# A graph attention kernel: two of 128 adjacency half loads issued as 120 and 8 partitions

## The chip, the cores and the metric

The kernel runs on one core of one Trainium2 chip. The metric is the device time of one execution in microseconds (us). The core has five engines (TensorE, VectorE, ScalarE, GpSimd and SyncE; in the profile PE with its weight loads PEld, DVE, ACT, POOL and SP) and sixteen DMA engines that move data between HBM and the on-chip memory.

## The reference

One layer of graph attention over 8192 nodes with 128 features. `adj` is an int32 matrix of 8192 x 8192, 256 MiB, in which about one entry in 2048 is 1, so a row has some four neighbours.

```python
h = jnp.maximum(_layernorm(x, axis=-1), 0.0)
s_i = h @ attn[:128]
s_j = h @ attn[128:]
e = leaky_relu(s_i + s_j.T, negative_slope=0.2)
e = e + jnp.where(adj > 0, 0.0, -1e9)
out = x + softmax(e, axis=1) @ h
```

## The kernel before

The rows are split into 64 tiles of 128 rows (`TILES`); row `64 p + t` lies on partition p of tile t. Two tiles make a pair (`PAIRS` = 32). The kernel first normalises `x`, writes a table of rows of h to HBM, and then streams the adjacency matrix once, finding each row's few neighbours and gathering only their rows of the table.

A tile of the adjacency matrix is loaded in two halves of 4096 columns. A half load is 128 partitions x 16,384 bytes, 2 MiB; there are 128 of them, numbered n = 2 t + h. They go into a ring of five slots, `adj_ring` (`HALVES` = 5, slot n % 5), each slot with a DMA semaphore of its own, `adj_in[n % 5]`, to which one DMA adds 16 when all of it has landed. All the half loads are issued by SyncE, in `load_pair` (L410 to 415), in order. Before load n it waits until ScalarE has signed half n - 5 (L413). On the same queue, in program order, stand the stores of the finished pairs (`store_pair`, L417 to 421).

ScalarE, in `sign_tile` (L606 to 615), waits for half n to land (L609), writes its sign as one byte per element into `sign_ring` (four slots), which frees the slot of `adj_ring`, and counts `signed` up. TensorE packs the signs into words in PSUM (`pack_tile`, L1366), VectorE finds the largest words of each chunk (L769) and from them the neighbours' numbers `near_id`; GpSimd gathers the neighbours' rows (`gather_pair`, L521, twelve indirect DMAs a pair), and VectorE scores, weighs and sums them (L906 to L957). Every eight pairs a list of rows with many neighbours is treated in a like manner (`near_m`, L532). After the last half has been signed comes a closing part: the last pairs, the rows without any neighbour (128 matmuls at L1442), and the last stores.

Of the kernel before, what the change touches and what calls it, by code (L numbers as in the profile page):

```python
# [5 lines left out]
def graph_attention_kernel(nc: bass.Bass, x: bass.AP, adj: bass.AP, attn: bass.AP, out: bass.AP):  # L6
# [6 lines left out]
    P = 128  # L13
# [3 lines left out]
    HALF = N // 2  # L17
# [15 lines left out]

    DIGITS = CHUNKS // 2
    HALVES = 5
    SHIFTS = [3 * (c // 2) + 2 * (c % 2) for c in range(CHUNKS)]
    EACH = sum(8 ** d for d in range(DIGITS)) * WORDS
    UNIT = 11.0
# [49 lines left out]

    def early_parts(k):
        return [c for c in range(LONE_PARTS[0]) if PART_AT[c] == k]  # L90

    table = nc.dram_tensor("h_table", [N + 1, COLS], fp32).ap()

# [3 lines left out]
    adj_t = adj.rearrange("(p t) c -> t p c", p=P)  # L97
# [3 lines left out]
    with ctx:  # L101
        def sb(name, shape, dt):
            return ctx.enter_context(nc.sbuf_tensor(name, shape, dt))
# [4 lines left out]
        def sem(name):  # L108
            return ctx.enter_context(nc.semaphore(name))

        adj_ring = sb("adj_ring", [P, HALVES, HALF], i32)
        sign_ring = sb("sign_ring", [P, 4, HALF], fp8)
# [179 lines left out]
        attn_in = sem("attn_in")  # L292
        adj_in = [sem(f"adj_in{i}") for i in range(HALVES)]
        consts = sem("consts")
# [107 lines left out]
        @block.sync  # L402
        def _(sp):
            for c in range(XC):
                sp.dma_start(x_all[:, c * XT:(c + 1) * XT, :], x_t[:, c * XT:(c + 1) * XT, :]).then_inc(x_in[c], 16)
                if c == 0:
                    sp.dma_start(attn_b[:, :], attn.rearrange("d o -> o d").broadcast_to([P, 2 * D])) \
                        .then_inc(attn_in, 16)

            def load_pair(p):  # L410
                for n in range(4 * p, 4 * p + 4):
                    if n >= HALVES:
                        sp.wait_ge(signed, n - HALVES + 1)  # L413
                    sp.dma_start(adj_ring[:, n % HALVES, :], adj_t[n // 2, :, (n % 2) * HALF:(n % 2 + 1) * HALF]) \
                        .then_inc(adj_in[n % HALVES], 16)

            def store_pair(g):  # L417
                sp.wait_ge(pair_mixed, g + 1)
                if g >= 2:
                    sp.wait_ge(stored[g % 2], 16 * (g // 2))  # L420
                sp.dma_start(out_t[:, 2 * g:2 * g + 2, :], x_all[:, 2 * g:2 * g + 2, :]).then_inc(stored[g % 2], 16)

            load_pair(0)
            load_pair(1)
            for p in range(2, PAIRS):
                load_pair(p)
                for g in MIXES.get(p - 2, []):
                    store_pair(g)
            for g in range(PAIRS - 4, BODY + 1):
                store_pair(g)  # L430

            sp.wait_ge(sizes_ready, 2)
            tiles = sp.value_load(far_tiles[0:1, 0:1], min_val=1, max_val=TILES)
            parts = sp.value_load(far_parts[0:1, 0:1], min_val=1, max_val=DC)
            with sp.Fori(0, tiles) as t:
                with sp.Fori(0, parts) as c:
                    sp.wait_ge(far_used, DC * t + c + 1)
                    sp.sem_inc(sp_passed, 1)
                    sp.dma_start(far_h, table[ds(c * DW + 1, DW), :].rearrange("(k q) c -> q k c", q=P)) \
                        .then_inc(far_h_in, 16)  # L440
                    sp.dma_start(far_adj, adj_t[ds(t, 1), :, ds(c * DW, DW)].rearrange("o p w -> (o p) w")) \
                        .then_inc(far_adj_in, 16)
                    sp.wait_ge(far_free, DC * t + c + 1)
                    sp.sem_inc(sp_passed, 1)
                    sp.dma_start(far_x, x_t[:, ds(t, 1), :].rearrange("p o d -> p (o d)")).then_inc(far_x_in, 16)

        @block.gpsimd
        def _(pool):
# [24 lines left out]
            for c in range(CHUNKS):  # L473
                nc.gpsimd.memset(code_mask[:, c:c + 1], 2 ** SHIFTS[c] * WORDS + WORDS - 1)
            nc.gpsimd.memset(fill[:, :], SKIP)
# [127 lines left out]
        def _(act):  # L603
            act.wait_ge(consts, 1)

            def sign_tile(t, halves=(0, 1)):  # L606
                for h in halves:
                    n = 2 * t + h
                    act.wait_ge(adj_in[n % HALVES], 16 * (n // HALVES) + 16)  # L609
                    if n >= 4:  # L610
                        act.wait_ge(packed, n - 3)
                    bytes_of = sign_ring[:, n % 4, :].rearrange("p (d i r) -> p d r i", d=DIGITS // 2, r=2)
                    nc.scalar.activation(bytes_of, adj_ring[:, n % HALVES, :].rearrange("p (d r i) -> p d r i", r=2, i=WORDS),  # L613
                                         ACT.Sign, bias=half_neg[:, :], saturate=False,
                                         accum_out=degree[:, t, h:h + 1]).then_inc(signed, 1)
# [45 lines left out]
            root_quarter(2)  # L661
            root_quarter(3)
            sign_tile(0)
            relu_quarter(2)
            sign_tile(1)
            def exp_lone(b, c):
                part = lone_p[b][c % len(lone_p[b])]
# [3 lines left out]
            def exp_step(p):  # L671
                for g in MIXES.get(p, []):
                    exp_pair(g)
                for c in early_parts(p - 1 - FIRST_STEP):
                    exp_lone(0, c)

            for p in range(1, PAIRS):
                sign_tile(2 * p, (0,))
                exp_step(p - 1)
                sign_tile(2 * p, (1,))  # L680
                sign_tile(2 * p + 1, (0,))
                if p >= SEG and p % SEG == DEEP_MIX:
                    exp_m(p // SEG - 1)
                sign_tile(2 * p + 1, (1,))
# [31 lines left out]
        def _(dve):  # L716
# [432 lines left out]
            def lone_add(c):  # L1149
                n = LONE_MARK + LONE_HOT + LONE_IDS  # L1150
                acc = lone_acc[0:LONE_CAP[0], :]
                dve.wait_ge(lone_summed[0], early_parts(c)[-1] + 1)
                if c == 0:
                    nc.vector.tensor_copy(acc, lone_sum[0]).then_inc(lone[0], 1)
                else:
                    dve.wait_ge(lone[0], n + c)
                    nc.vector.tensor_tensor(acc, acc, lone_sum[0], ALU.add).then_inc(lone[0], 1)
# [29 lines left out]
            def lone_close(p):  # L1187
                for c in early_parts(p - FIRST_STEP):
                    lone_part(0, c)
# [358 lines left out]
```

## Time and profile before

| | us |
|---|---|
| median of 3 runs | 821.86 |
| lowest, highest | 820.19, 822.15 |
| span of the profiled execution | 819.9 |
| VectorE busy | 615.3 |
| ScalarE busy | 534.3 |
| GpSimd busy | 505.0 |
| TensorE busy | 379.5 |

The span is the time from the first to the last instruction of one profiled execution. Its views are: busy time by engine and stretch, with the mean busy share of the sixteen DMA engines and the GB/s that they moved; the chain of work that ended last, followed back from the end; who waited for whom; the DMA queues and issues; and the instructions in order of time. In them "x" before a number is a count. An idle time is put down to what ended it. The profile doesn't tell the sixteen DMA engines apart: it gives their mean share and their sum.

### The profile page before, as it was taken

The numbers are of one execution on the slowest core, as the hardware profiler recorded it, in microseconds if no ns is written. First come the engines' busy times: TensorE is split into PE (matmuls) and PEld (weight loads), VectorE is DVE, ScalarE is ACT, GpSimd is POOL, SyncE is SP. The second block draws the span as 40 slices with busy tenths as digits, with TensorE's granted clock in tenths as the row PEclk, the third lists the DMA queues.
The fourth block names the chain that finished last, engine by engine and source line by source line (L and its number), as shares of the span: only waits on it lengthen the run. The fifth ranks groups of instructions, "written<-read, shape, count | busy, mean of one in ns | idle before, by whom it ended". The sixth has DMA issues, their size and how long they took to land.

```text
span 819.9 us, 6412 instructions
## 1 busy us (share of the span) xinstructions
PE 379.5 (46%) x1378; PEld 171.4 (21%) x1378; DVE 615.3 (75%) x2028; ACT 534.3 (65%) x410; POOL 505.0 (62%) x526
## 2 busy tenths in 40 slices
PE   1546334444444344344343434444434546653765
PEld 1322011111111011111111101111111215431654
DVE  6898298677768667797778666697689799897831
ACT  4975676676676666766766666676676677764620
POOL 6720777755457767665547677555557667655771
PEclk9776665555555555555555555655555556766768
DMA  8999999999999999999999999999999999981210
GB/s 341 402 411 415 392 404 408 406 414 413 409 407 410 408 405 410 406 410 410 412 406 407 408 406 407 411 410 413 412 413 409 408 411 407 409 348 43 53 37 4
DMA packets 39719, 301.59 MB, mean 368 GB/s; under 512 B 10682, under 2 KB 17149, under 8 KB 22272
## 3 DMA queue, kind: packets, MB, share of 16 engines
q1 hardware_dynamic: 24032, 277.04, 83.1%
q0 software_dynamic: 15360, 23.88, 8.5%
q10 hardware_dynamic: 288, 0.26, 0.1%
q8 instruction: 11, 0.18, 0.1%
q14 instruction: 28, 0.23, 0.1%
HBM read 303.76 MB, written 8.98 MB: 381 GB/s over the span
## 4 chain that ended last, share of the span: by engine, by line
DMA 76%; issue 11%; DVE 5%; ACT 4%; PE 3%; POOL 0%; DVEq 0%; ACTq 0%
DMA adj_ring<-in_adj_dram 75%; ACT sign_ring L613 3%; PE words L1442 2%; DVE one_hot L724 1%; ACT h_all L625 1%; PE words L1406 1%; DMA x_all<-in_x_dram 1%; PE words L1366 0%; DVE cand L769 0%; DVE adj_ring L1142 0%; DVE adj_ring L1138 0%; DVE adj_ring L1146 0%; PE words L1516 0%; POOL out_dram L562 0%; ACT terms L620 0%
## 5 line engine op out<-in xcount | busy, mean ns | idle before, releaser
L613 ACT ACTIVATE sign_ring<-adj_ring,half_neg 128x4096 fp8e3<-128x4096 int32 x128 | 474.9, 3710 | 217.1 <-DMA adj_ring<-in_adj_dram 215.4
L521 POOL DMA_INDIRECT near<-h_table,near_id x384 | 391.8, 1020 | 235.4 <-issue 122.8
L1366 PE MATMUL words<-sign_ring,pack_w 128*128 128x512 bf16 x512 | 225.2, 592 | 354.8 <-ACT sign_ring L613 354.8
L769 DVE MAX8 cand<-words 128x8 f32<-128x256 f32 x256 | 90.9, 417 | 115.4 <-PE words L1366 115.4
L1366 PEld LDWEIGHTS words<-sign_ring,pack_w 128*128 128x128 bf16 x512 | 55.0, 127 | 521.9 <-ACT sign_ring L613 451.6
L954 DVE TENSOR_REDUCE sums<-terms 128x128 f32<-128x1024 f32 x58 | 112.2, 1934 | 2.0
L532 POOL DMA_INDIRECT near_m<-h_table,id_m x64 | 64.5, 1008 | 19.5 <-issue 19.2
L949 DVE TENSOR_TENSOR terms<-near,weight 128x512 f32<-128x512 f32 (+1 forms) x87 | 73.4, 871 | 0.0
L1357 PE MATMUL words<-place,place_w 128*128 128x512 bf16 x128 | 62.1, 586 | 3.6 <-DVE key L861 3.6
L1392 PEld LDWEIGHTS listing<-cand,one_hot 128*128 128x128 f32 x128 | 33.6, 321 | 10.9 <-issue 7.7
L1347 PE MATMUL listing<-h_all 128*1 128x128 f32 x128 | 19.1, 322 | 22.8 <-ACT h_all L625 22.8
L1392 PE MATMUL listing<-cand,one_hot 128*128 128x34 f32 x128 | 28.0, 362 | 0.2 <-DVE one_hot L865 0.2
L613 ACT ACTIVATION_READ_ACCUMULATOR sign_ring<-adj_ring,half_neg 128x1 f32 x128 | 23.8, 186 | 0.0
L1442 PE MATMUL rank<-h_all,x_all 128*64 128x129 f32 x128 | 21.1, 344 | 4.6 <-DVE key L861 4.6
L786 DVE TENSOR_TENSOR terms<-cand_i,code_mask 128x512 int32<-128x512 int32 x32 | 22.2, 693 | 1.1
L957 DVE SCALAR_TENSOR_TENSOR x_all<-sums,inv,x_all 128x128 f32<-128x128 f32 x58 | 20.4, 352 | 2.1
L643 ACT ACTIVATE adj_ring<-ident,adj_ring 128x128 f32<-128x128 f32 x48 | 14.4, 387 | 11.1 <-DVE adj_ring L969 11.1
L755 DVE TENSOR_TENSOR near<-h_all,terms 128x2048 f32<-128x2048 f32 x8 | 21.5, 2686 | 0.0
L1442 PEld LDWEIGHTS rank<-h_all,x_all 128*64 128x64 f32 x128 | 20.3, 182 | 4.9 <-DVE key L861 4.9
L498 POOL TENSOR_SCALAR h_all<-x_all,terms 128x128 f32<-128x128 f32 x16 | 13.0, 830 | 11.7 <-DVE terms L741 11.7
L625 ACT ACTIVATE h_all<-x_all,terms 128x128 f32<-128x128 f32 x48 | 18.8, 479 | 2.1 <-DVE terms L741 2.1
L906 DVE TENSOR_SCALAR score<-near,h_all 128x8 f32<-128x8 f32 x32 | 7.3, 228 | 17.1 <-DMA near<-h_table,near_id 17.1
(271 smaller groups left out, 524.3 us busy)
## 6 DMA issues: line engine op xcount, KB each, us to landing
adj_ring<-in_adj_dram SPq DMA_DIRECT2D x128, 2048.0 KB, 24.6
near<-h_table,near_id POOLq DMA_INDIRECT x384, 6.4
h_table<-h_all POOLq DMA_DIRECT2D x4, 1056.0 KB, 14.7
x_all<-in_x_dram SPq DMA_DIRECT2D x4, 1024.0 KB, 9.4
out_dram<-x_all SPq DMA_DIRECT2D x30, 128.0 KB, 23.9
near_m<-h_table,id_m POOLq DMA_INDIRECT x64, 6.4
out_dram<-x_all ACTq DMA_DIRECT2D x2, 128.0 KB, 2.5
adj_ring<-h_table SPq DMA_DIRECT2D x1, 132.0 KB, 2.6
```

Source lines behind the costliest of these rows:

```text
L521: pool.indirect_dma_start(out=near[:, p % RING, k, :], out_offset=None, in_=table, in_offset=bass.IndirectOffsetOnAxis(ap=near_id[:, p % I ...
L532: pool.indirect_dma_start(out=near_m[:, k, :], out_offset=None, in_=table, in_offset=bass.IndirectOffsetOnAxis(ap=id_m[:, k:k + 1], axis=0 ...
L613: nc.scalar.activation(bytes_of, adj_ring[:, n % HALVES, :].rearrange("p (d r i) -> p d r i", r=2, i=WORDS), ACT.Sign, bias=half_neg[:, :] ...
L625: nc.scalar.activation(h_all[:, t, 0:D], x_all[:, t, :], ACT.Relu, bias=shift[:, t:t + 1], scale=rstd[:, t:t + 1]).then_inc(h_ready, 1)
L769: last = nc.vector.max(out=cand[:, p % 2, t % 2, 8 * q:8 * q + 8], in_=words[t % 3][:, q * PART:(q + 1) * PART])
L786: nc.vector.tensor_tensor(codes[:, :, :, :].rearrange("p a w c -> p (a w) c"), cand_i[:, :, :].rearrange("p a w -> p (a w)").unsqueeze(2). ...
L949: nc.vector.tensor_tensor(terms[:, at, :], near[:, e, slots, 0:D], weight[:, g % 2, weights].unsqueeze(2).broadcast_to([P, at.stop - at.st ...
L954: nc.vector.tensor_reduce(sums[:, a, :], terms[:, :, :].rearrange("p k d -> p d k"), AX.X, ALU.add).then_inc(mixing, 1)
L1357: nc.tensor.matmul(at[:, k * BANK:(k + 1) * BANK], place_w[:, :], place[:, k * BANK:(k + 1) * BANK], start=True, stop=False)
L1366: last = nc.tensor.matmul(at[:, k * BANK:(k + 1) * BANK], pack_w[:, d, :], twins[:, o + k * BANK:o + (k + 1) * BANK], start=False, stop=(d ...
L1392: last = nc.tensor.matmul(listing[:, 0:REC], one_hot[:, p % 2, a, :], cand[:, p % 2, a, :], start=(p % SEG == 0 and a == 0), stop=(p % SEG ...
L1442: last = nc.tensor.matmul(lone_sum[b], part[:, k * e:(k + 1) * e], h_all[:, c * lt + k, 0:ONE + 1], start=(first and k == 0), stop=(final ...
```

## The change

Half loads 52 and 104 are issued as two DMAs each: one of partitions 0 to 119 and one of partitions 120 to 127, with the same columns, the same slot and the same semaphore. Each adds 16 to the semaphore, so the value that ScalarE waits for is no longer 16 a load but 16 for each DMA of that slot up to and with load n (`landed`). The other 126 loads, their order and all the compute instructions are the same.

```diff
     HALVES = 5
+    SPARED = (52, 104)
+    WIDE = 120
...
+    def landed(n):
+        return 16 * sum(2 if k in SPARED else 1 for k in range(n % HALVES, n + 1, HALVES))
...
                     if n >= HALVES:
                         sp.wait_ge(signed, n - HALVES + 1)
-                    sp.dma_start(adj_ring[:, n % HALVES, :], adj_t[n // 2, :, (n % 2) * HALF:(n % 2 + 1) * HALF]) \
-                        .then_inc(adj_in[n % HALVES], 16)
+                    columns = slice((n % 2) * HALF, (n % 2 + 1) * HALF)
+                    for rows in ((slice(0, WIDE), slice(WIDE, P)) if n in SPARED else (slice(0, P),)):
+                        sp.dma_start(adj_ring[rows, n % HALVES, :], adj_t[n // 2, rows, columns]) \
+                            .then_inc(adj_in[n % HALVES], 16)
...
-                    act.wait_ge(adj_in[n % HALVES], 16 * (n // HALVES) + 16)
+                    act.wait_ge(adj_in[n % HALVES], landed(n))
```

## Rows read from the trace of the kernel before

**Rows 1.** The page's chain that ended last: share of the span by line.

```profile
DMA adj_ring<-in_adj_dram 75%; ACT sign_ring L613 3%; PE words L1442 2%; DVE one_hot L724 1%; ACT h_all L625 1%; PE words L1406 1%; DMA x_all<-in_x_dram 1%; PE words L1366 0%; DVE cand L769 0%; DVE adj_ring L1142 0%; DVE adj_ring L1138 0%; DVE adj_ring L1146 0%; PE words L1516 0%; POOL out_dram L562 0%; ACT terms L620 0%
```

**Rows 2.** The same chain in order of time: start us, us, what.

```profile
93.30 24.48 DMA adj_ring<-in_adj_dram
117.80 3.81 ACT sign_ring L613 x2
...
719.76 3.81 ACT sign_ring L613 x2
723.59 23.35 DMA adj_ring<-in_adj_dram
746.96 3.81 ACT sign_ring L613 x2
...
810.92 0.98 POOL out_dram L562
```

**Rows 3.** ScalarE in order of time, 463 to 500: start, duration, idle before.

```profile
475.08 3.71 ACT L613 ACTIVATE sign_ring<-adj_ring,half_neg 128x4096 fp8e3<-128x4096 int32 x1 [1.72 <-DMA adj_ring<-in_adj_dram]
...
482.00 3.71 ACT L613 ACTIVATE sign_ring<-adj_ring,half_neg 128x4096 fp8e3<-128x4096 int32 x1 [3.11 <-DMA adj_ring<-in_adj_dram]
...
487.42 3.71 ACT L613 ACTIVATE sign_ring<-adj_ring,half_neg 128x4096 fp8e3<-128x4096 int32 x1 [1.51 <-DMA adj_ring<-in_adj_dram]
...
492.89 3.71 ACT L613 ACTIVATE sign_ring<-adj_ring,half_neg 128x4096 fp8e3<-128x4096 int32 x1 [1.67 <-DMA adj_ring<-in_adj_dram]
```

**Rows 4.** Groups of instructions by line, 120 to 720: the signs.

```profile
L613 ACT ACTIVATE sign_ring<-adj_ring,half_neg 128x4096 fp8e3<-128x4096 int32 x107 | 397.1, 3711 | 191.3 <-DMA adj_ring<-in_adj_dram 189.6 <-PE words L1366 1.7
```

**Rows 5.** Busy time by stretches: engines, granted PE clock, DMA share, GB/s.

```profile
core 0: us, PE busy (x) PEld busy (x) DVE busy (x) ACT busy (x) POOL busy (x), PEclk, DMA share, GB/s
60.00:100.00 40.00, 18.74 (x56) 7.06 (x57) 22.78 (x86) 23.91 (x13) 14.93 (x16) 0.63 1.01 404
100.00:200.00 100.00, 42.83 (x116) 14.49 (x114) 78.60 (x259) 68.05 (x41) 67.81 (x66) 0.55 1.01 409
...
500.00:600.00 100.00, 42.40 (x116) 13.91 (x116) 74.64 (x261) 68.06 (x44) 55.49 (x57) 0.55 1.01 411
600.00:700.00 100.00, 52.70 (x199) 26.62 (x199) 90.43 (x274) 71.18 (x43) 72.82 (x70) 0.54 1.01 409
700.00:734.00 34.00, 18.02 (x75) 11.44 (x76) 31.05 (x104) 23.17 (x16) 21.59 (x22) 0.67 1.01 406
```

**Rows 6.** The page's DMA issues: count, KB each, median us to landing.

```profile
adj_ring<-in_adj_dram SPq DMA_DIRECT2D x128, 2048.0 KB, 24.6
```

**Rows 7.** DMA from 726 to 750 us in 40 slots of 0.6.

```profile
GB/s 420 410 368 364 404 394 495 410 375 387 403 336 354 311 200 167 128 63 41 32 133 27 90 60 25 90 27 99 27 71 27 56 27 214 67 46 21 21 92 0
```

**Rows 8.** Busy time by stretches around the last loads, columns as in rows 5.

```profile
724.00:728.00 4.00, 1.50 (x4) 0.29 (x2) 3.74 (x19) 3.02 (x3) 3.09 (x4) 0.50 1.02 408
728.00:732.00 4.00, 1.92 (x6) 0.72 (x6) 3.62 (x14) 1.81 (x3) 1.70 (x2) 0.50 1.00 403
732.00:736.00 4.00, 3.40 (x18) 3.40 (x19) 3.83 (x21) 3.19 (x3) 0.02 (x1) 0.55 0.69 280
736.00:738.00 2.00, 2.00 (x19) 1.71 (x18) 1.90 (x8) 1.51 (x1) 1.08 (x2) 1.00 0.13 51
...
sum 24.00, PE 14.11 PEld 8.17 DVE 22.62 ACT 16.66 POOL 13.75; mean PE 1.57 PEld 0.91 DVE 2.51 ACT 1.85 POOL 1.53
```

**Rows 9.** DMA queues from 474 to 484: packets, MB, share of 16 engines.

```profile
q1 hardware_dynamic: 263, 3.74, 92.6%
q0 software_dynamic: 245, 0.29, 8.3%
q14 instruction: 1, 0.01, 0.2%
```

**Rows 10.** The same from 480 to 500.

```profile
q1 hardware_dynamic: 656, 7.65, 93.9%
q0 software_dynamic: 458, 0.48, 7.0%
q14 instruction: 1, 0.01, 0.1%
```

**Rows 11.** The page's DMA queues of code: packets, MB, share.

```profile
q8 instruction: 11, 0.18, 0.1%
q14 instruction: 28, 0.23, 0.1%
```

**Rows 12.** One line's instructions, L414: ns of one, minimum, median, maximum.

```profile
L414 SPq DMA_DIRECT2D adj_ring<-in_adj_dram x128: 327/328/629, 3.3 to 723.6; - x128
```

**Rows 13.** What SyncE's queue waited for: us in total, times, longest.

```profile
SPq L414 <- ACT sign_ring L613: 639.7, 121, 22.8
```

**Rows 14.** The head of the page.

```profile
span 819.9 us, 6412 instructions
```

## Prediction

> **What bounds the kernel now.** I read the chain of waits first. Three quarters of the span is one line, the landing of `adj_ring` [rows 1]; in order of time it alternates between about 24 us of waiting for a half load and one sign on ScalarE that frees the next slot of the ring [rows 2]. The sign is short beside the wait, 3.71 us of every period [rows 3]. From the sign at 117.80 to the one at 719.76 ScalarE signs 107 halves [rows 4], so 106 periods take 601.96 us, 5.68 us each [rows 2].
>
> The next view is the busy time by stretches. From 60 to 734 us the sixteen DMA engines are occupied all the time (share 1.01) and move 404 to 411 GB/s. VectorE is busy some 75 to 79 us of 100, and 90 of 100 from 600 to 700 [rows 5]. So what the load stage waits for is the DMA engines' own work, not an issue, a buffer or a compute engine. A load is issued 24.6 us before it lands (median) [rows 6], more than four periods of 5.68 us: an engine has a queue of transfers ahead of it, and one that falls behind isn't starved, it just stays behind.
>
> The third view is the end of the loads, and it is the one that matters here. Twelve slots of 0.6 us show near 400 GB/s; between 734 and 737 the rate falls to 32, and from there to 745.8 the floor is 27 GB/s, with short peaks of gathers on top [rows 7]. One sixteenth of 408 is 26, so that floor is one engine working alone, for about 9 us, while fifteen have finished. The mean share says the same: 1.02, 1.00, 0.69, then 0.13 from 736 to 738 [rows 8]. The last sign can't start before 746.96 [rows 2]. Since all sixteen get equal parts of each load, this engine carries something besides. The signs show what: from 475.08 to 482.00 the period is 6.92 us, 1.24 over the mean [rows 3], and the stretch from 474 to 484 holds one 8 KB packet of queue 14, instruction code [rows 9]. In 480 to 500, behind that one, there is another such packet [rows 10], and the periods stay at 5.42 and 5.47 us [rows 3]. So a code fetch lies on one engine, and only some of them on the engine that is last. Seven or eight at 1.24 us make the 9 us; the page counts 28 and 11 fetches in all [rows 11]. The pace of the kernel is that of this one engine, which I call the last engine.
>
> After 746.96 comes a chain of 73 us to the end with no adjacency load in it [rows 2]. What the last load gains or loses moves that chain whole.
>
> **The change part by part.** *Issue.* Two more DMAs on SyncE's queue. One takes 0.33 us [rows 12], so 0.66 us in all. SyncE waits 639.7 us for signs [rows 13]; behind each issue stand only the next loads and the stores of results, and a load is issued some 20 us before it is due. Cost on the path: nothing, hidden by the queue of transfers; without that cover it would be 0.66 us.
>
> *The wait.* ScalarE waits for 16 more on the semaphore of that slot. It is the same instruction with another number, for the same bytes. Nothing, as long as both parts land together.
>
> *The wide part.* 120 rows of 16 KB divide evenly over fifteen engines, eight rows each, and not over sixteen. I take it that one engine gets none. An engine alone moves 27 GB/s [rows 7], so a row of 16,384 bytes costs it 0.61 us and eight rows 4.85 us. If the one left out is the last engine, it is relieved of 2 x 4.85 = 9.7 us.
>
> *The narrow part.* Eight rows on eight engines, one each: 0.61 us for each of those eight, twice, 1.2 us. If the last engine is among them, 1.2 us on the path.
>
> The Trainium skill, "DMA: Bandwidth & Descriptors", section "Why a DMA increments its semaphore by 16 and not by 1", says that a DMA from SyncE runs on the largest number of engines up to 16 that divides its slowest dimension, and that these are the lowest-numbered; by that, 120 rows leave out the highest-numbered engine and the eight rows use the lowest eight. No run here shows it yet. The section "Latency and other measured facts" calls engines 7 and 15 usually slower, which would make the one left out the right one; the trace agrees that one engine is last, but has no number for it, and ties its lag to code fetches. "SBUF — State Buffer", "Door 1: The DMA port swizzle", speaks against the change: eight partitions in two groups of four share a port of some 27 GB/s, and a full load gives each engine its own port. By that rule the upper bound above would be the likely value, and the sum for an unrelieved last engine would be 12.1 us instead of 6.1.
>
> **The sum.** No row names the engine that is last, or the one that 120 rows leave out. They are two of sixteen, and the fetches are spread over more than one engine [rows 3, 9, 10], so I don't count on their being the same. Then the last engine keeps its eight rows in both wide parts, gets one more row in each narrow part (1.2 us), and writes among others' partitions (4.9 us): 6.1 us later at the last sign, and at the end. The profiled execution, span 819.9 us [rows 14], stands 2.0 us under the median of 821.86, the launch around it included. 821.9 + 6.1 = 828.0 us.
>
> **The rivals.** *A, the forecast: the last engine isn't relieved.* Price 0 to +12.1 us (1.2 + 10.9), so 821.9 to 834.0. For it: nothing in the profile points at the one left out. Against it: the relief of 9.7 us fits the 9 us of lag.
>
> *B, the last engine is the one left out, and the sharing costs little.* It would be done 9.7 us earlier; then the second-latest sets the end, which [rows 7] puts 9 us ahead, plus up to 1.2 for the narrow rows. Gain 8 to 9 us; VectorE, busy 22.6 of the 24 us before 748 [rows 8], may keep back 1 or 2 of it. So 812.9 to 815. It decides when the wide part costs the other fifteen less than some 2 us: they have only those 9 us in hand. For it speaks the size of the lag; against it, that sixteen engines could be meant.
>
> *C, left out, but the sharing gives it back.* The other fifteen are 9 us ahead and pay 1.2 + 4.9 to 1.2 + 10.9 us; the sum is -3 to +3 us against now, 819 to 825.
>
> *D, the change doesn't do what it says:* both parts are spread over all engines anyway, or the eight rows lie on engines that have slack. Then 821.9, within A's and C's range.
>
> **How the numbers follow.** Two executions of this kernel can be told apart from about 0.3%, 2.5 us, so "same" is 819.4 to 824.4. A has a chance of 0.55, of which 0.12 within 2.5 us (little sharing, D with it) and 0.43 slower. B has 0.27, all faster. C has 0.18: 0.04 faster, 0.09 same, 0.05 slower. Together faster 0.31, same 0.21, slower 0.48. The likeliest case is A, 828.0; its own range is 822 to 834. B is too likely to leave out, so the range goes down to 812.5; up it goes to 834.
>
> **What would show it.** The view of the end of the loads, as in [rows 7], tells the cases apart. In B the floor of 27 GB/s is gone or under 2 us and the last sign starts near 738 to 739. In A the floor is as long or longer and the last sign starts at 748 or later. In C there is no floor, but the fall comes late, near 745 to 749. Sharing would show as longer periods of the signs around halves 52 and 104 (near 322 and 616 us): in A one period of 5.68 us becomes 8 to 11, in C the periods lengthen only where the slack is used up. The wait of ScalarE for `adj_ring`, and nothing on VectorE or TensorE, should take up the difference. The prediction is wrong if the left-out engine is the last one, or if the tail behind the last load doesn't move with it.

## The result and the profile after

The changed kernel takes 846.22 us (843.86 to 850.58, 4 runs) against 821.63 us (820.19 to 822.15, 4 runs): 1.0301 of the time before, 95% interval 1.0278 to 1.0324. It is 24.6 us slower, and above the range of the prediction. The profiled execution has a span of 842.1 us, 22.2 us over that of before.

The page first: the GB/s of the span in 40 slices of 21 us, and the count, MB and share of SyncE's DMA queue.

```profile
GB/s 345 405 405 419 401 406 405 410 411 411 410 402 412 407 363 291 408 413 414 415 415 405 408 409 407 412 411 412 369 259 353 406 407 402 408 352 46 50 37 5
q1 hardware_dynamic: 24046, 277.04, 82.9%
```

Two dents stand in a row that is flat otherwise, at slices 15 and 16 (295 to 337 us) and 29 to 31 (589 to 653 us), where half loads 52 and 104 pass. The queue has as many MB as before and 14 packets more. One load on sixteen engines has 128 rows and 16 semaphore writes; in 120 + 8 it has the same 128 rows and 15 + 8 writes, 7 more, 14 for two loads. (The column split below, with two more DMAs of 128 rows, has 288 packets more, 144 each.) So the wide part did run on fifteen engines and the narrow one on eight, as the Trainium skill, "DMA: Bandwidth & Descriptors", section "Why a DMA increments its semaphore by 16 and not by 1", has it.

The same dents by stretches (columns as in rows 5: busy time of each engine, granted PE clock, DMA share, GB/s):

```profile
290.00:312.00 22.00, 9.27 (x25) 3.26 (x26) 14.52 (x53) 14.73 (x10) 15.02 (x15) 0.50 1.03 399
312.00:326.00 14.00, 4.06 (x10) 1.02 (x9) 4.27 (x13) 6.05 (x4) 10.91 (x11) 0.50 1.00 219
326.00:340.00 14.00, 3.24 (x10) 0.64 (x7) 8.59 (x30) 6.43 (x4) 7.49 (x8) 0.62 1.00 370
...
606.00:624.00 18.00, 4.26 (x13) 1.93 (x14) 14.69 (x54) 8.33 (x7) 12.24 (x12) 0.55 1.03 220
```

The DMA share stays at 1.00 while the rate is 219 GB/s, against the 404 to 411 of [rows 5]: on the mean every engine is occupied, and its packets take nearly twice as long. The kernel before has 412 GB/s from 312 to 326. In slots of 1.2 us, first from 296 to 344 and then from 592 to 640, the dents have clear edges:

```profile
GB/s 393 442 381 419 412 397 406 385 424 437 423 311 365 188 219 235 249 234 232 198 203 190 229 219 236 257 253 352 386 401 366 410 404 392 410 414 363 443 385 394
```
```profile
GB/s 425 384 412 393 424 387 422 387 410 408 405 396 257 248 218 194 264 225 218 186 221 147 226 200 151 230 200 207 345 442 339 402 385 373 403 378 355 363 410 374
```

The rate is halved for 14 slots, 16.8 us from 311.6, and for 16 slots, 19.2 us from 606.4. From 290 to 340 the changed kernel moves 22 x 399 + 14 x 219 + 14 x 370 = 17.0 thousand GB/s x us, that is 17.0 MB; at the 409 of a normal stretch it would be 20.5. The missing 3.4 MB are 8.4 us of work.

ScalarE's signs show where it lands (start, duration, idle before); these are halves 50 to 53:

```profile
310.45 3.71 ACT L620 ACTIVATE sign_ring<-adj_ring,half_neg 128x4096 fp8e3<-128x4096 int32 x1 [1.22 <-DMA adj_ring<-in_adj_dram]
320.70 3.71 ACT L620 ACTIVATE sign_ring<-adj_ring,half_neg 128x4096 fp8e3<-128x4096 int32 x1 [6.45 <-DMA adj_ring<-in_adj_dram]
332.52 3.71 ACT L620 ACTIVATE sign_ring<-adj_ring,half_neg 128x4096 fp8e3<-128x4096 int32 x1 [8.02 <-DMA adj_ring<-in_adj_dram]
337.48 3.71 ACT L620 ACTIVATE sign_ring<-adj_ring,half_neg 128x4096 fp8e3<-128x4096 int32 x1 [1.05 <-DMA adj_ring<-in_adj_dram]
```

In the kernel before they start at 310.88, 316.37, 322.20 and 327.89. So sign 50 is on time, sign 51 is 4.3 us late although load 51 isn't cut, sign 52 is 10.3 and sign 53 9.6 us late. The delay then shrinks to 8.4 us by sign 99. Around the second cut it goes to 15.7 (sign 102), 19.0, 26.0 (sign 104) and settles at 22.9, which is also the delay of the last sign (769.87 against 746.96).

The end of the loads, 750 to 774 us in slots of 0.6, to be set against [rows 7]:

```profile
GB/s 443 350 440 416 483 292 359 338 167 157 82 27 27 27 34 27 27 27 77 84 27 123 7 108 27 99 27 65 34 25 31 210 93 27 46 0 113 0 97 0
```

The floor of 27 GB/s is still there. It runs from 756.6 to 768.6, 12.0 us; counted in the same way it was 8.4 us before, from 737.4 to 745.8 in [rows 7]. At 27 GB/s one engine is alone as before, and it is further behind. The 73 us behind the last sign [rows 2] are 72.2 us now: the delay is passed on whole. ScalarE's wait for `adj_ring` takes up the difference: 239.2 us in all, was 215.4. TensorE's and VectorE's longer waits follow from it: TensorE waits 379.9 us for signs (was 354.8), and VectorE 126.9 us for TensorE's words (was 115.4).

### The profile page after: what moved, and what is told of

Its sections match the earlier page's. It is cut to its first block, busy times and chain, and to the rows that moved or that the text cites. A ratio compares the mean times of both kernels' runs of the same rounds, so it can differ in the third digit from the quotient of the medians.

```text
span 842.1 us, 6395 instructions
## 1 busy us (share of the span) xinstructions
PE 371.0 (44%) x1359; PEld 170.2 (20%) x1378; DVE 614.7 (73%) x2028; ACT 534.2 (63%) x410; POOL 503.9 (60%) x526
## 4 chain that ended last, share of the span: by engine, by line
DMA 70%; issue 13%; DVE 5%; POOL 4%; ACT 3%; PE 3%; DVEq 0%; POOLq 0%; ACTq 0%
DMA adj_ring<-in_adj_dram 66%; POOL near L528 4%; ACT sign_ring L620 2%; DVE near L762 2%; PE words L1449 2%; DMA h_table<-sums 2%; DMA near<-h_table,near_id 1%; DVE one_hot L731 1%; ACT h_all L632 1%; PE words L1413 1%; DMA x_all<-in_x_dram 1%; DVE h_all L767 0%; PE words L1373 0%; DVE cand L776 0%; PE words L1523 0%
## 5 line engine op out<-in xcount | busy, mean ns | idle before, releaser
L620 ACT ACTIVATE sign_ring<-adj_ring,half_neg 128x4096 fp8e3<-128x4096 int32 x128 | 474.9, 3710 | 239.2 <-DMA adj_ring<-in_adj_dram 239.2
L1373 PE MATMUL words<-sign_ring,pack_w 128*128 128x512 bf16 x511 | 220.9, 583 | 380.1 <-ACT sign_ring L620 379.9
L776 DVE MAX8 cand<-words 128x8 f32<-128x256 f32 x256 | 90.9, 417 | 126.9 <-PE words L1373 126.9
L539 POOL DMA_INDIRECT near_m<-h_table,id_m x64 | 64.4, 1006 | 19.5 <-issue 19.2
L1364 PE MATMUL words<-place,place_w 128*128 128x512 bf16 x110 | 55.3, 588 | 7.8 <-DVE key L868 4.4
L1399 PEld LDWEIGHTS listing<-cand,one_hot 128*128 128x128 f32 x128 | 32.7, 314 | 10.6 <-issue 7.2
L1354 PE MATMUL listing<-h_all 128*1 128x128 f32 x128 | 19.1, 322 | 24.6 <-ACT h_all L632 24.6
L793 DVE TENSOR_TENSOR terms<-cand_i,code_mask 128x512 int32<-128x512 int32 x32 | 22.2, 693 | 1.1
L964 DVE SCALAR_TENSOR_TENSOR x_all<-sums,inv,x_all 128x128 f32<-128x128 f32 x58 | 20.4, 352 | 2.1
L632 ACT ACTIVATE h_all<-x_all,terms 128x128 f32<-128x128 f32 x48 | 18.8, 479 | 2.2 <-DVE terms L748 2.2
L913 DVE TENSOR_SCALAR score<-near,h_all 128x8 f32<-128x8 f32 x32 | 7.2, 224 | 17.5 <-DMA near<-h_table,near_id 17.5
```

What stands on the lines that cost most here:

```text
L539: pool.indirect_dma_start(out=near_m[:, k, :], out_offset=None, in_=table, in_offset=bass.IndirectOffsetOnAxis(ap=id_m[:, k:k + 1], axis=0 ...
L632: nc.scalar.activation(h_all[:, t, 0:D], x_all[:, t, :], ACT.Relu, bias=shift[:, t:t + 1], scale=rstd[:, t:t + 1]).then_inc(h_ready, 1)
L776: last = nc.vector.max(out=cand[:, p % 2, t % 2, 8 * q:8 * q + 8], in_=words[t % 3][:, q * PART:(q + 1) * PART])
L1364: nc.tensor.matmul(at[:, k * BANK:(k + 1) * BANK], place_w[:, :], place[:, k * BANK:(k + 1) * BANK], start=True, stop=False)
L1373: last = nc.tensor.matmul(at[:, k * BANK:(k + 1) * BANK], pack_w[:, d, :], twins[:, o + k * BANK:o + (k + 1) * BANK], start=False, stop=(d ...
L1399: last = nc.tensor.matmul(listing[:, 0:REC], one_hot[:, p % 2, a, :], cand[:, p % 2, a, :], start=(p % SEG == 0 and a == 0), stop=(p % SEG ...
```

## The experiments

They ran in four sessions, for which the record names four chips (15, 3, 0 and 6). On each the kernel before takes 834 to 835 us instead of 821.6. It falls behind the first measurement step by step: 7.2 us at sign 50, 15.1 at sign 99 and 16.4 at the end. The medians are set against the runs of the kernel before in the same session (835.15, 835.05, 835.05 and 834.07 us). The signs are set against one profile of it, taken on chip 3. The table gives how late a sign starts against that profile, in us. Also with no cut these levels wander, by up to 8 us (a kernel with no cut stands at -8.2 at sign 101). Over four or five signs with no cut they move by 2.7 us at most. So the jumps across a cut count, not the levels.

| kernel | sign 50 | 54 | 101 | 106 | 127 |
|---|---|---|---|---|---|
| changed kernel (a2_after) | 2.8 | 13.4 | 8.6 | 20.4 | 21.5 |
| split by columns (e3) | -0.3 | 1.2 | -2.2 | -0.6 | -0.1 |
| 120 alone (e4) | -0.9 | 7.3 | 1.3 | 15.1 | 15.2 |
| 112 + 16 (e6) | -0.2 | 8.0 | 6.6 | 18.8 | 18.3 |
| 64 + 64 (e5) | 0.4 | 12.1 | 7.0 | 19.6 | 18.8 |
| other source rows (e7) | 0.5 | 8.8 | 4.2 | 18.2 | 17.5 |
| only 52 cut (e1) | 1.5 | 11.3 | 3.1 | 2.8 | 3.3 |
| only 104 cut (e2) | 0.3 | -0.6 | -3.3 | 11.1 | 10.3 |

**The reference profile.** The kernel before, unchanged.

> The kernel before, unchanged, profiled on the chip of the experiments, so that the signs of the others can be set against it half by half. 835 us if the chip is the one of the first experiments, 822 if it is like that of the first measurement.

836.79 us, span 835.0.

**The changed kernel on this chip.** No edit.

> The changed kernel itself on the chip of the experiments (where the kernel before takes 835 us). If both cuts have the price seen in the single cuts there: signs late by 11 us behind 52, falling to some 3 to 5 before 102, then 13 us more; 851 to 857 at the end. The difference to the kernel without the eight rows (late by 15 us at the end) is the price of the narrow part: 1 to 4 us.

857.33 us, ratio 1.0251 (1.0192 to 1.0309). The price is the same in kind and size, 23.3 us. Before the second cut comes, the delay has fallen to 6.3 (sign 99) and 8.6 us (sign 101) and not to 3 to 5, and the second jump is 11.8 us and not 13; both are within what the levels wander by.

**Two DMAs, but equal parts.**

```diff
-    WIDE = 120
+    CUT = 3840
...
-                    for rows in ((slice(0, WIDE), slice(WIDE, P)) if n in SPARED else (slice(0, P),)):
-                        sp.dma_start(adj_ring[rows, n % HALVES, :], adj_t[n // 2, rows, columns]) \
+                    base = (n % 2) * HALF
+                    for a, b in (((0, CUT), (CUT, HALF)) if n in SPARED else ((0, HALF),)):
+                        sp.dma_start(adj_ring[:, n % HALVES, a:b], adj_t[n // 2, :, base + a:base + b]) \
```

> Half loads 52 and 104 are again issued as two DMAs each on one semaphore, but split by columns: 128 partitions x 3840 columns and 128 partitions x 256 columns. Same bytes, same number of issues, same waits, and every engine keeps its equal part and its partitions. Theory 1 (the price is that fifteen engines write partitions that others write as well): no change against the kernel before, 821.6 within 1 us. Theory 2 (the price is the second issue, its semaphore or the shared wait): the whole 24.6 us of the changed kernel comes back, 846.

836.92 us against 835.15, ratio 1.0026 (1.0003 to 1.0048). The second issue, the shared semaphore and the longer wait cost 1.8 us for both loads together (0.3 to 4.0 by the interval), and a part of that may be the short rows of 1 KB. That is over the 1 us of theory 1, and far from the 24.6 of theory 2, which falls.

**The wide part alone.**

```diff
-        return 16 * sum(2 if k in SPARED else 1 for k in range(n % HALVES, n + 1, HALVES))
+        return 16 * sum(1 for k in range(n % HALVES, n + 1, HALVES))
...
-                    for rows in ((slice(0, WIDE), slice(WIDE, P)) if n in SPARED else (slice(0, P),)):
+                    for rows in ((slice(0, WIDE),) if n in SPARED else (slice(0, P),)):
```

> Of half loads 52 and 104 only partitions 0 to 119 are loaded; partitions 120 to 127 of these two halves keep what the slot held before (so the output of those rows is another one). Theory 1 (the price lies in the 120-partition DMA): 840 to 846, the signs behind half 52 late by 7 to 10 us and behind half 104 by 18 to 23. Theory 3 (the eight rows of the narrow DMA, eight engines on few partitions, are the costly part): 822 to 830.

852.71 us, ratio 1.0206 (1.0168 to 1.0243). The 120 rows carry 17.6 us, a little under the 18.4 to 24.4 of theory 1, and the second jump left the signs 15 us late and not 18 or more. The changed kernel is 23.3 us over its own runs of the kernel before, so the eight rows add 5.7. That is more than their bytes (131 KB a load, 0.3 us at 408 GB/s) and more than the 1 to 4 expected, and a quarter of the price.

**Sixteen engines, other sets.** Cut at 112: seven rows and one row for each of sixteen engines.

```diff
-    WIDE = 120
+    WIDE = 112
```

> The two half loads are cut at partition 112 instead of 120: 112 = 16 x 7 and 16 = 16 x 1 rows, so all sixteen engines have equal parts and none is left out, but the parts are no longer the sets of partitions of a 128-row load. Theory 1 (sharing of partitions): as slow as the changed kernel or nearly, 835 to 850, with the rate halved for some 15 us around both halves. Theory 4 (the price is that one engine is left out and fifteen carry more): no loss, 821.6 within 2 us.

854.89 us, ratio 1.0232 (1.0194 to 1.0270). The queue has 32 packets more than before: both parts have sixteen semaphore writes, so they ran on all sixteen engines. No engine is left out and none has a row more, and the price is there. So it isn't the unequal load.

**Halves of the partitions.** The same edit with 64.

> The two half loads are cut into 64 and 64 partitions. All sixteen engines have four rows in each, but each part covers only half of the partitions. Theory 1 (engines that write partitions of the same group share its rate): the rate falls to about half around both loads and the signs are late by 8 to 15 us at each. If only the unequal split into fifteen mattered: no delay.

857.84 us, ratio 1.0261 (1.0223 to 1.0299), again with 32 packets more. The stretch from 322 to 336 us in the reference, the column split, 112 + 16, 64 + 64 and the one with other source rows, in this order and each from its own profile (columns as above):

```profile
322.00:336.00 14.00, 6.10 (x16) 1.50 (x16) 7.50 (x37) 8.06 (x6) 10.34 (x11) 0.62 1.01 391
```
```profile
322.00:336.00 14.00, 4.99 (x14) 1.38 (x13) 6.39 (x32) 7.71 (x5) 9.95 (x10) 0.62 1.01 352
```
```profile
322.00:336.00 14.00, 4.40 (x12) 1.09 (x10) 3.37 (x17) 3.80 (x2) 9.79 (x10) 0.50 1.02 224
```
```profile
322.00:336.00 14.00, 2.34 (x6) 0.62 (x7) 0.86 (x6) 4.10 (x4) 9.14 (x10) 0.50 1.00 196
```
```profile
322.00:336.00 14.00, 4.68 (x12) 1.23 (x12) 3.92 (x19) 4.20 (x4) 9.97 (x10) 0.50 1.00 217
```

Whenever the rows are cut, the rate is 196 to 224 GB/s with all engines occupied (206 for the changed kernel itself in the same stretch); when the columns are, it is 352, a tenth under the reference's 391. "SBUF — State Buffer", section "Door 1: The DMA port swizzle", of the Trainium skill says that 64 partitions reach eight of sixteen ports of about 27 GB/s, 218 GB/s together. The 196 of the 64 + 64 cut is a tenth under that, and the 217 to 224 of the other cuts sit at the same value. Which ports the engines reach at a time in those cuts no view shows.

**Other rows in HBM.**

```diff
-                        sp.dma_start(adj_ring[rows, n % HALVES, :], adj_t[n // 2, rows, columns]) \
+                        sp.dma_start(adj_ring[rows, n % HALVES, :], (adj[P * (n // 2):P * (n // 2) + P, :][rows, columns] if n in SPARED else adj_t[n // 2, rows, columns])) \
```

> As the changed kernel, but the two cut loads read rows of the matrix that follow each other in HBM (row pitch 32 KB) instead of every 64th row (pitch 2 MB); it computes two half tiles from the wrong rows. Theory 1 (the engines share the SBUF side: partitions written at the same moment): as late as the changed kernel, 9 to 10 and 13 to 15 us. Theory 5 (the rows of one engine collide in HBM because of the 2 MB pitch, now that another set of rows goes together): little or no delay.

856.13 us, ratio 1.0234 (1.0174 to 1.0294), with jumps of 8.4 and 14.0 us. The pitch of the source isn't the cause. With the column split (e3) and the cut at 112 (e6) this leaves the destination: which engine writes which partitions. That is an argument by elimination, since no view separates the engines.

**One cut at a time.** `SPARED = (52,)`, `(104,)`, `(20,)` and `(127,)`.

> Only half load 52 is cut into 120 and 8, load 104 is one DMA. If each cut load has its own price: the signs behind half 52 are late by 9 to 10 us and stay so to the end, 831. If the 14 us of the second one in the changed kernel come from the first one's after-effects (engines further apart), the end is the same 831, and a kernel with only load 104 cut would be late by 9 to 10 as well and not by 14.

> Only half load 104 is cut into 120 and 8. If the price grows with how far the DMA engines have drifted apart (by half 104 the last one is 9 us behind), the signs behind it are late by 13 to 15 us although nothing happened at 52. If the larger second price of the changed kernel came from the first cut, they are late by 9 to 10.

> Only half load 20 is cut, where the DMA engines have hardly drifted apart. If the price grows with the drift: 3 to 7 us late behind it. If it is the same for each cut: 9 to 10. A theory in which the cut relieves the last engine would have it earlier by up to 5 us at the end.

> Only the very last half load, 127, is cut into 120 and 8. When the last engine comes to it, the other fifteen have been done for some 9 to 13 us. If the price is that the last engine's own rows of the cut load meet other engines' writes: nobody is left to meet, 0 to 2 us late. If the price is that the engines ahead write, with their part of the cut load, the partitions on which the last engine still works for earlier halves: signs 125 to 127 late by 4 to 10 us in spite of that.

Only 52: 842.48 us, 1.0094 (1.0059 to 1.0129). Only 104: 848.09, 1.0138 (1.0074 to 1.0201). Only 20: 839.49, 1.0045 (1.0021 to 1.0069). Only 127: 844.63, 1.0124 (1.0085 to 1.0163). The jump across the cut is 9.8 us at 52 and 14.4 us at 104 with nothing at 52. So the larger second price isn't an after-effect of the first cut. At 20 the jump is 8.8 us (1.5 late at sign 18, 10.3 at 22), where I had expected 3 to 7, since the engines should hardly have drifted apart there. At 127 it is 10.6 us (from -4.6 at sign 123 to 6.0). A price that grows with the drift fits the first three and not the last, behind which no load follows; how far the engines are apart was measured at no cut. Most of the price is there at half 20 already.

What stays at the end is another matter. Against the reference profile the delay of the cut at 20 shrinks from 10.3 to 2.0 us by the last sign, and that of the cut at 52 from 11.3 to 3.3. But the seven kernels with no cut up to half 103 also gain 0.8 to 6.1 us on this profile between signs 54 and 99, so much of this is the reference's own. The medians against their own sessions are the better measure: 4.4, 7.3, 13.0 and 10.6 us for the cuts at 20, 52, 104 and 127, against jumps of 8.8, 9.8, 14.4 and 10.6. Of the cut at 20 about half is recovered (1.8 to 5.8 us are left by the interval); for the later ones the intervals don't tell what is left from the whole jump. How an early delay is recovered is open.

The cut at 127 shows that loads that aren't cut are held up too. Signs 124 to 127 of the reference and then of this kernel:

```profile
747.73 3.71 ACT L613 ACTIVATE sign_ring<-adj_ring,half_neg 128x4096 fp8e3<-128x4096 int32 x1 [2.17 <-DMA adj_ring<-in_adj_dram]
752.92 3.71 ACT L613 ACTIVATE sign_ring<-adj_ring,half_neg 128x4096 fp8e3<-128x4096 int32 x1 [1.28 <-DMA adj_ring<-in_adj_dram]
757.96 3.71 ACT L613 ACTIVATE sign_ring<-adj_ring,half_neg 128x4096 fp8e3<-128x4096 int32 x1 [1.24 <-DMA adj_ring<-in_adj_dram]
763.39 3.71 ACT L613 ACTIVATE sign_ring<-adj_ring,half_neg 128x4096 fp8e3<-128x4096 int32 x1 [1.63 <-DMA adj_ring<-in_adj_dram]
```
```profile
744.67 3.71 ACT L620 ACTIVATE sign_ring<-adj_ring,half_neg 128x4096 fp8e3<-128x4096 int32 x1 [3.72 <-DMA adj_ring<-in_adj_dram]
755.59 3.71 ACT L620 ACTIVATE sign_ring<-adj_ring,half_neg 128x4096 fp8e3<-128x4096 int32 x1 [7.01 <-DMA adj_ring<-in_adj_dram]
761.87 3.71 ACT L620 ACTIVATE sign_ring<-adj_ring,half_neg 128x4096 fp8e3<-128x4096 int32 x1 [2.48 <-DMA adj_ring<-in_adj_dram]
769.39 3.71 ACT L620 ACTIVATE sign_ring<-adj_ring,half_neg 128x4096 fp8e3<-128x4096 int32 x1 [3.72 <-DMA adj_ring<-in_adj_dram]
```

From sign 124 to 127 the reference takes 15.66 us, this kernel 24.72. Of the 9.1 us more, 5.7 fall before sign 125 and 7.0 before sign 126, two loads that aren't cut. Only the last 2.1 us come with load 127 itself. A reading that fits is that the engines ahead are in load 127 by then and write, with their part of it, partitions that slower engines are still filling for 125 and 126. That they are the same partitions is argued, since no view shows an engine's own writes.

**Which engine is last.** The kernel before with one more DMA behind load 104, which copies k x 8 rows of 16 KB from HBM to HBM and touches no partition; k = 3, 4, 8, 12 and 15. It was meant to run on k engines. The cut for k = 15; in the others 15 and 120 are k and 8 k:

```diff
+    spare = nc.dram_tensor("spare", [15, 8 * HALF], i32).ap()
...
+        spare_in = sem("spare_in")
...
+                    if n == 104:
+                        sp.dma_start(spare.rearrange("k (m c) -> k m c", m=8), adj[0:120, 0:HALF].rearrange("(k m) c -> k m c", m=8)) \
+                            .then_inc(spare_in, 16)
...
+            sp.wait_ge(spare_in, 16)
```

> As the last, with 3 x 8 rows on three engines. Late by 4.9 us if the pacing engine is one of the three, within 1 us if not. Late with four and not with three would name the fourth engine; late with neither leaves the fifth to the sixteenth.

> As the last, with 4 x 8 rows, so on four engines. If the pacing engine is one of the four that such a DMA uses, late by 4.9 us; if it is another, within 1 us.

> Kernel before with 8 x 8 rows copied within HBM behind load 104, on eight engines. With four engines there was no delay, with fifteen about 5 us. A delay of 4.9 us or more from sign 105 on puts the pacing engine among the fifth to eighth; none puts it among the ninth to fifteenth.

> As the last with 12 x 8 rows on twelve engines. A delay of 4.9 us or more here and none with eight puts the pacing engine among the ninth to twelfth; none here either, among the thirteenth to fifteenth.

> The kernel before with one DMA more behind half load 104: 15 x 8 rows of 16 KB are copied from HBM to a spare place in HBM, which divides over fifteen engines like the wide part, but touches no partition. If the engine that paces the kernel is one of these fifteen, the signs behind half 104 and the end are late by 4.9 us or somewhat more. If it is the one left out, it isn't delayed, and with 5 to 7 us of slack in the others the end stays within 1 us.

The jump from sign 104 to sign 106 is 1.4, 1.5, 2.5, 3.8 and 6.3 us for k = 3, 4, 8, 12 and 15; the medians are 835.04, 835.93, 837.76, 837.13 and 838.88 us, which is 0.0, 0.9, 3.7, 3.1 and 3.8 over the kernel before. The expected picture, nothing and then 4.9 us at once, isn't there, and the packets say why: the edit didn't confine the copy to k engines. SyncE's queue has 36, 48, 80, 112 and 135 packets more than before. Less the 24, 32, 64, 96 and 120 rows that leaves 12, 16, 16, 16 and 15 semaphore writes, one for each engine. So an engine of the copy had 2, 2, 4, 6 and 8 rows, and at 0.61 us a row [rows 7] that is 1.2, 1.2, 2.4, 3.6 and 4.9 us, close to the jumps. The first leaves four engines out, but its 1.4 us is within what the signs wander by. The last leaves one out. Its delay speaks for the last engine being among its fifteen, since the one left out has nothing more to do; but 1.97 MB at 408 GB/s are 4.8 us as well, so it isn't proof. These runs don't name the engine. They show another thing: fifteen engines with eight rows each and no partition to write cost 6.3 us, and the rate doesn't halve (404 GB/s from 624 to 636 and 396 from 636 to 648), where as many rows sent to partitions 0 to 119 halve it.

## Why the prediction was wrong

**The bound of the load stage: right.** The delay of the last sign, 22.9 us, is the delay of the profiled execution (22.2), and in both dents the DMA share is 1.00 or more. (VectorE's 75 to 79 us of 100 were read too narrowly: it is busy 68 to 80 in the stretches from 100 to 600. Nothing hangs on it.)

**Issue and wait: put at nothing, measured 1.8 us (0.3 to 4.0).** The column split has both.

**The parts on fifteen and eight engines: right.** The packet count shows them.

**The last engine isn't relieved: right as far as shown.** The floor of 27 GB/s went from 8.4 to 12.0 us; with 9.7 us taken off that engine and nothing else changed it would have gone. That it is the same engine as before isn't shown. Rival B, 812.9 to 815, is out. So is C as it was put, with at most 3 us over the time before; that an engine was relieved and a much larger price hid it is made unlikely only by the copy on fifteen engines.

**The cause of the lag: supported, not tested.** The prediction tied it to code fetches from a single period. In the kernel before, 12 of the 108 periods between signs 19 and 127 are longer than 6.3 us, and each of the 12 holds a packet of queue 14; the other 96 are 5.54 us on the mean, and some hold such a packet too. No run takes a fetch away.

**The mixing of rows and engines: the right mechanism, the wrong size.** This term failed. The prediction put it at 0 to 10.9 us for both loads and took 4.9, which with 1.2 for the narrow rows made 6.1; the signs jumped by 10 and 14.5 us, 24.6 us at the end. The upper bound was built from the cut load alone: the last engine's own eight rows and one at half speed, 5.45 us a load. It left out that the cut load slows loads that aren't cut. The runs show this: sign 51 is 4.3 us late, and with only load 127 cut, 5.7 us are lost before sign 125. The rate was halved for 16.8 and 19.2 us, not for the 9.6 us that the 2.10 MB of the cut load take at 219 GB/s. The reading of it is that sixteen engines don't reach a load together. From the moment when the first of them enters the cut load until the last has left it, somebody writes partitions that another is writing, and the rate is halved. An estimate: the last engine is 8.4 us behind at the end of the loads, so, if that grows evenly, 3.4 us at load 52 and 6.9 at 104. With the 9.6 us this gives 13.0 and 16.5 us, some 3 us short of both dents. The spread of the engines itself wasn't measured.

**The rule that was set aside.** The port rule of the Trainium skill ("SBUF — State Buffer", "Door 1: The DMA port swizzle") stood in the prediction as what would make the upper bound the likely value. The halved rate of the runs agrees with it. The middle of the bounds was taken with no row near it; where a resource is known to be full (share 1.01 at 408 GB/s), the full price was the better guess. But also the sum with the full price, 12.1 us, is half of what was measured.

**The forecast of the profile: half right.** I had expected one period of 8 to 11 us near halves 52 and 104. Near 52 there were two, 10.25 and 11.82 us, and near 104 three, 11.20, 9.11 and 12.74. The longer floor, the late last sign and the wait on ScalarE came as forecast for A.

## What to carry to other kernels

In a stream of 128-partition loads that keeps all DMA engines occupied, don't cut one by its rows. In all four cuts tried here, one such load halved the rate for itself and for its neighbours, in the changed kernel for 17 and 19 us; cut by its columns, two loads cost 1.8 us together. To take work off a late engine, look for a way that leaves the sets of partitions alone; 8 to 14 us a load is as much as the whole lag of 8.4 us or more. To put a DMA on few engines, count its packets before reading anything from it: of five copies meant for k engines only one ran on k. And when the price of a shared resource is bounded, count the traffic of everybody who meets the odd transfer, not only the late engine's own.

## What was not expected of the hardware

- A sixteen-way equal split is no protection: 112 + 16 partitions ran at 224 GB/s and 64 + 64 at 196, where the kernel before has 391; 120 + 8 ran at 219 in the first measurement, with 412 before.
- The DMA share says nothing of it: 1.00 at 219 GB/s. The GB/s have to be read beside it.
- The source's row pitch, 2 MB or 32 KB, made no clear difference to a cut load (206 and 217 GB/s, 23.3 and 21.1 us over the kernel before), and whole loads with the 2 MB pitch ran at 408.
- The jump at one cut load was 8.8 us at half 20, 9.8 at 52, 14.4 at 104 and 10.6 at 127, and the medians were 4.4, 7.3, 13.0 and 10.6 us over the kernel before. Why half of the earliest one is recovered is open.
